# Weights that land in the place of their low parts, and VectorE's order in time mixing, in a one-layer RWKV and feed-forward kernel

## The chip, the cores and the metric

The kernel runs on one core of one Trainium2 chip. The metric is the device time of one execution in microseconds; lower is better. The five compute engines are named as the profile names them: PE (TensorE), DVE (VectorE), ACT (ScalarE), POOL (GpSimd), SP (SyncE, which here issues DMAs). An SBUF tile of 128 partitions by 512 fp32 elements is 256 KB.

## What is computed

```
x  = layernorm(x0) (no gain)            # then, on that x:
h  = LN(x)*g1 + b1;  hh = h shifted by one token (first row 0)
k  = (h*mk + hh*(1-mk)) @ Wk.T          # v with mv and Wv, r with mr and Wr
wkv = a / b of the first step of the recurrence (from k, v, tm_first)
x1 = x + (sigmoid(r) * wkv) @ Wo.T
h2 = LN(x1)*g2 + b2;  hh2 = h2 shifted
kv = silu((h2*ck + hh2*(1-ck)) @ Wkey.T) @ Wval.T
x2 = x0 + x1 + sigmoid((h2*cr + hh2*(1-cr)) @ Wcr.T) * kv
out = x2 + (silu(z @ Wg.T) * (z @ Wu.T)) @ Wdown.T,   z = layernorm(x2)
```

There are 2048 tokens, 512 features, and an inner width of 2048. Wr, Wk, Wv, Wo and Wcr are 512 x 512, all fp32.

## The kernel before, in words

**Precision.** Each fp32 operand of a matmul is split into two parts. The high part is what ScalarE's copy into a float32r tile leaves (`ACT.Copy`); the low part is the raw value minus the high part, a `tensor_tensor` subtract. Each product takes three passes: high x high, high x low, low x high (lines 488 to 490). A 512 x 512 weight matrix is four tiles ("items") of 128 x 512 and so costs four high copies on ScalarE and four low subtracts on GpSimd.

**Tokens** are worked in four blocks `b` of 512. Time mixing and the receptance of channel mixing come first (to about 285 us); then 48 "units" of the key, value and gated feed-forward products run to the end, and the change does not touch their code.

**TensorE's order in time mixing** is written out by hand: first_norm1 (transposes), receptance(0), key(0), norm1(1), value(0), and for b = 1 to 3: receptance(b), output(b-1), key(b), norm1(b+1) (or norm2(0)), value(b). Then norm2(1), channel_receptance(0), norm2(2), output(3), channel_receptance(1), norm2(3), channel_receptance(2) and (3). Each product is 48 matmuls of 128 x 512. `banks` A hold transposes, banks B hold products.

**The chain of one operand** (kind r, k, v, y or cr, block b): ScalarE's `rest_of` writes the shifted share from bank A into one of four ring tiles `made` (line 744); VectorE's `mix` adds the own share (lines 1097, 1099; the second is the first column alone, which takes its shifted share from `edge`); ScalarE's `operand_hi` makes the high part (line 733); GpSimd's `operand_lo` the low part (line 1409) and with it frees the ring tile. y has gated_value (line 1132) in the place of rest_of and mix.

**Every engine works strictly in the order of its own list**, and waits are semaphores. `receptance_gate` (sigmoid of bank B, line 761) frees bank B for the next product: key(0) waits for gate(0), and output(0) for gate(1). `wkv_weight(b)` is ScalarE's relu and two exps (lines 768 to 773) with VectorE's two products (lines 1121, 1124); it frees bank B for value(b).

**Weights.** Wr and Wk (items 0 to 7) are loaded to `held` at the start. Wv, Wo and Wcr go through a staging area of two tiles (`load`, line 378): SP loads item n once `item_done` says that GpSimd has made the low part of item n-2. ScalarE makes the high parts of Wv right after the mixing of k0, those of Wo after the mixing of r1, those of Wcr in block 3 before wkv_weight(3). `item_done` counts all low parts in one semaphore.

**The last token of a block** (`last_token`) goes to `edge`: four copies of one column from the bank (line 1078), a product with `rest_g` (line 1080) and an addition of the vector beta (line 1083), for all mixes at once.

**VectorE's order**: constants, first_norm1, mix r0, norm1_stats(1), mix k0, norm1(1), mix v0, last_token(0,0), norm1_stats(2), back_to_first, wkv_weight(0), norm1(2), mix r1, norm1_stats(3); then for each b: gated_value(b-1), mix k_b, mix v_b, last_token, (b = 1: norm1(3)), output(b-1), norm2_stats(b-1), wkv_weight(b), norm2(b-1), mix r_(b+1). GpSimd makes the inverse roots (`norm1`, `norm`: lines 1421, 1425) between its low parts.

## Time and profile before

| | us |
|---|---|
| median of 3 runs (1127.1 to 1129.96) | 1128.62 |
| the profiled execution's own time | 1127.89 |
| its span (first to last instruction) | 1126.1 |
| PE busy in it | 1063.3 (94%) |
| VectorE, ScalarE, GpSimd busy | 636.6, 485.6, 551.5 |

The profiled execution ran 1.8 us longer than its span and 0.7 us under the median. PE busy says how long a matmul was in flight, at whatever clock; its idle time is 63 us, most of it in the first 100 us.

### The profile page before, as it was taken

To read this page: it belongs to the slowest core of one execution; us is meant where nothing else is said; L and a number is where in the kernel's file an instruction comes from. 1 tells how busy PE (TensorE), PEld (TensorE's weight loads), DVE (VectorE), ACT (ScalarE), POOL (GpSimd) and SP (SyncE) were. 2 spreads that over 40 slices of the span, in tenths; PEclk is the share of its full clock that TensorE was granted. 3 is DMA by queue.
4 is the path that set the end of the run, shared out by engine and by line. 5 is a ranking of instruction groups with operands and counts; after the bars stand their busy time and mean duration, and the time that the engine had idled before them with its cause. 6 is when DMAs were issued, how large, how long until landed. Compare 5 with 4: busy or idle time off the path is not lost. (4 is left out here: it accounts for less than half of the span.)

```text
span 1126.1 us, 13091 instructions
## 1 busy us (share of the span) xinstructions
PE 1063.3 (94%) x4704; PEld 875.0 (78%) x4704; DVE 636.6 (57%) x1073; ACT 485.6 (43%) x807; POOL 551.5 (49%) x460
## 2 busy tenths in 40 slices
PE   4597999998999999999999999999998999999998
PEld 3476888877788887888877788887876788888887
DVE  6466574787344647556338556676659433333334
ACT  5456756766544345243334433333334222222221
POOL 5754537544575664355336465564644433333322
PEclk9798999999999999999999899999999999999999
DMA  6110203336853344635232266664446364444422
GB/s 245 38 38 0 39 1 64 68 125 223 326 181 128 123 168 149 188 126 191 85 102 100 98 224 225 224 208 142 162 181 208 94 222 150 143 147 150 146 80 75
DMA packets 45233, 157.18 MB, mean 140 GB/s; under 512 B 4080, under 2 KB 4208, under 8 KB 40560
## 3 DMA queue, kind: packets, MB, share of 16 engines
q1 hardware_dynamic: 30000, 108.10, 27.8%
q0 software_dynamic: 15168, 48.24, 14.3%
q8 instruction: 38, 0.62, 0.2%
q14 instruction: 27, 0.22, 0.1%
HBM read 97.60 MB, written 58.72 MB: 139 GB/s over the span
## 5 line engine op out<-in xcount | busy, mean ns | idle before, releaser
L1220 DVE TENSOR_TENSOR resid<-bank,resid 128x512 f32<-128x512 f32 x240 | 164.8, 689 | 244.3 <-PE bank L490 242.7
L499 PE MATMUL bank<-combo,left 128*128 128x512 f32 x672 | 264.1, 393 | 12.7 <-ACT bank L904 7.2
L1452 POOL TENSOR_TENSOR inner<-made,inner 128x512 fp32r<-128x512 f32 x128 | 167.5, 1330 | 219.8 <-ACT inner L859 219.5
L500 PE MATMUL bank<-combo,left 128*128 128x512 f32 x672 | 262.6, 391 | 0.0
L501 PE MATMUL bank<-combo,left 128*128 128x512 f32 x672 | 262.3, 390 | 0.0
L488 PE MATMUL bank<-right,inner 128*128 128x512 f32 x512 | 199.3, 389 | 0.0
L489 PE MATMUL bank<-right,inner 128*128 128x512 f32 x512 | 199.2, 389 | 0.0
L490 PE MATMUL bank<-right,inner 128*128 128x512 f32 x512 | 199.2, 389 | 0.0
L1430 POOL TENSOR_TENSOR left<-quart,left 128x512 fp32r<-128x512 f32 x96 | 116.7, 1237 | 104.8 <-ACT left L824 53.3
L499 PEld LDWEIGHTS bank<-combo,left 128*128 128x128 f32 x672 | 126.8, 189 | 42.9 <-ACT bank L904 8.5
L501 PEld LDWEIGHTS bank<-combo,left 128*128 128x128 f32 x672 | 126.8, 189 | 26.7
L500 PEld LDWEIGHTS bank<-combo,left 128*128 128x128 f32 x672 | 126.9, 189 | 25.9
L1447 POOL TENSOR_TENSOR right<-tall_staged,right 128x512 fp32r<-128x512 f32 x64 | 85.6, 1347 | 56.7 <-ACT right L837 56.7
L488 PEld LDWEIGHTS bank<-right,inner 128*128 128x128 f32 x512 | 96.1, 188 | 20.3 <-POOL inner L1452 0.4
L490 PEld LDWEIGHTS bank<-right,inner 128*128 128x128 f32 x512 | 96.1, 188 | 20.1
L489 PEld LDWEIGHTS bank<-right,inner 128*128 128x128 f32 x512 | 96.1, 188 | 19.9
L1409 POOL TENSOR_TENSOR operand<-made,operand 128x512 fp32r<-128x512 f32 x64 | 81.9, 1359 | 57.3 <-ACT operand L733 57.3
L880 ACT ACTIVATE made<-bank 128x512 f32<-128x512 f32 x64 | 38.0, 593 | 150.4 <-PE bank L501 150.4
L488 PE MATMUL bank<-operand,weights 128*128 128x512 f32 x176 | 70.1, 398 | 14.2 <-ACT held L761 13.5
L1097 DVE SCALAR_TENSOR_TENSOR made<-bank,whole_g,made 128x511 f32<-128x511 f32 x64 | 47.6, 744 | 55.8 <-ACT made L744 55.8
L868 ACT ACTIVATE made<-bank 128x512 f32<-128x512 f32 x64 | 37.5, 586 | 95.9 <-PE bank L501 95.9
L859 ACT ACTIVATE inner<-made 128x512 fp32r<-128x512 f32 x128 | 77.2, 628 | 2.7 <-ACT made L868 0.4
(130 smaller groups left out, 1464.2 us busy)
## 6 DMA issues: line engine op xcount, KB each, us to landing
kept_left<-left SPq DMA_DIRECT2D x24, 1792.0 KB, 8.1
left<-kept_left POOLq DMA_DIRECT2D x24, 1024.0 KB, 7.1
left<-kept_left POOLq DMA_DIRECT2D x24, 768.0 KB, 5.0
tall_staged<-tall SPq DMA_DIRECT2D x64, 256.0 KB, 3.3
quart<-wide SPq DMA_DIRECT2D x24, 512.0 KB, 4.2
raw<-kept SPq DMA_DIRECT2D x32, 256.0 KB, 6.4
resid<-x POOLq DMA_DIRECT2D x4, 1024.0 KB, 9.2
kept<-resid SPq DMA_DIRECT2D x4, 1024.0 KB, 5.8
```

What stands on the lines that cost most here:

```text
L488: pe.matmul(acc, left(0), right(0), start=first, stop=False)
L489: pe.matmul(acc, left(0), right(1), start=False, stop=False)
L490: return pe.matmul(acc, left(1), right(0), start=False, stop=last)
L499: pe.matmul(acc[:], hi, combo[:, c, k, 0, :], start=fresh and k == 0, stop=False, skip_group_check=True)
L500: pe.matmul(acc[:], hi, combo[:, c, k, 1, :], start=False, stop=False, skip_group_check=True)
L501: mm = pe.matmul(acc[:], lo, combo[:, c, k, 0, :], start=False, stop=k == 1, skip_group_check=True)
L859: act.activation(inner[:, h % 4, i, 0, :], made_at(n), ACT.Copy).then_inc(inner_hi, 1)
L1220: dve.tensor_tensor(tile, A[s][:], tile, ALU.add).then_inc(added, 1)
L1409: pool.tensor_tensor(place(kind, b, k, 1), made[:, (n + k) % RING, :], place(kind, b, k, 0).bitcast(F32), ALU.subtract).then_inc(op_lo, 1)
L1430: lo = pool.tensor_tensor(left[u % 2][:, 1, a[0]:a[0] + n, :], quart[:, a[0] + 1:a[0] + 1 + n, :], left[u % 2][:, 0, a[0]:a[0] + n, :].bit ...
L1447: pool.tensor_tensor(right[:, g % 2, i, 1, :], tall_staged[i][:], right[:, g % 2, i, 0, :].bitcast(F32), ALU.subtract).then_inc(right_lo, 1)
L1452: pool.tensor_tensor(inner[:, h % 4, i, 1, :], made_at(n), inner[:, h % 4, i, 0, :].bitcast(F32), ALU.subtract).then_inc(inner_lo, 1)
```

## The change

- The raw tile of every weight item is loaded straight into the place of its low part in `weights` (`landed`, the same memory as fp32). ScalarE reads it there, and the low part is written over it. The staging area and its waits are gone. SP issues the 16 items of Wr, Wk, Wv before block 1's tokens, Wo after them, then blocks 2 and 3. Wcr takes the rows of Wr and is loaded once receptance(3) is done.
- The low parts of Wk, of Wv and of the last tile of Wr move from GpSimd to VectorE. Those of Wo stay on GpSimd, at the same place; those of Wcr on GpSimd move from before `norm(BLOCKS + 2)` in block 3 to just before the low part of cr0, and its high parts on ScalarE from before wkv_weight(3) to behind it.
- `item_done` becomes one semaphore for each matrix.
- The small vectors are loaded second, behind the first token tile; `constants()` runs inside first_norm1.
- VectorE's order: the r-tile and Wk's first two tiles around mix r0 and mix k0, then Wk's other two, norm1_stats(1), Wv's four, norm1(1), mix v0, last_token, wkv_weight(0), norm1_stats(2), back_to_first, mix r1. norm1(2) and norm1(3) move to between mix k_b and mix v_b of blocks 1 and 2; norm1_stats(3) moves behind last_token of block 1.
- `last_token` makes each edge column in one instruction from the bank (12 or 8 tiny ones in the place of 6).
- ScalarE does channel_receptance(1) before, and no longer behind, the high parts of T2 and of unit 0's left factors.

```diff
-STAGES = 2
-EARLY = ITEM_V
+ROWS = 16
...
+        landed = at("landed", AT_WEIGHTS, [P, ROWS, 2, 512])
...
         def landing(item):
-            return early(item) if item < EARLY else staging[:, item % STAGES, :]
+            return landed[:, item % ROWS, 1, :]
...
-            def load(item, source):
-                if item >= EARLY + STAGES:
-                    sp.wait_ge(item_done, item - STAGES + 1)
-                sp.dma_start(staging[:, item % STAGES, :], source).then_inc(staged[item % STAGES], 16)
+            def load(items):
+                for item in items:
+                    sp.dma_start(landing(item), wts[item]).then_inc(w_loaded[item], 16)
...
-            for n in range(SUBS):
+            sp.dma_start(resid[:, 0, 0], x_blocks[0][:, 0, :]).then_inc(x_first[0], 16)
+            sp.dma_start(vec[:], vectors).then_inc(vec_loaded, 16)
+            for n in range(1, SUBS):
                 sp.dma_start(resid[:, 0, n], x_blocks[0][:, n, :]).then_inc(x_first[n], 16)
-            sp.dma_start(vec[:], vectors).then_inc(vec_loaded, 16)
             sp.dma_start(ident[:], identity).then_inc(ident_loaded, 16)
-            load_early(range(ITEM_R, ITEM_K))
+            load(range(ITEM_R, ITEM_O))
             sp.dma_start(resid[:, 1], x_blocks[1]).then_inc(x_loaded[0], 16)
-            load_early(range(ITEM_K, ITEM_V))
+            load(range(ITEM_O, ITEM_CR))
             for b in range(2, BLOCKS):
                 sp.dma_start(resid[:, b], x_blocks[b]).then_inc(x_loaded[b - 1], 16)
-            for item in range(ITEM_V, ITEMS):
-                load(item, wts[item])
+            sp.wait_ge(r_psum, KT * BLOCKS)
+            load(range(ITEM_CR, ITEMS))
```

On ScalarE:

```diff
-                if b + 1 == BLOCKS:
-                    act.wait_ge(r_psum, KT * BLOCKS)
-                    matrix_hi(ITEM_CR, ROW_CR)
                 wkv_weight(b)
                 if b + 1 < BLOCKS:
                     mixed("r", b + 1)
+            matrix_hi(ITEM_CR)
             mixed("cr", 0)
...
             combo_hi_of(0, T3)
+            channel_receptance(1)
             combo_hi_of(0, T2)
             unit_left_hi(0, 0)
             unit_left_hi(0, 1)
-            channel_receptance(1)
```

On VectorE:

```diff
                 for k in range(KT):
                     dve.wait_ge(transposed, KT * b + k + 1)
-                    dve.tensor_copy(last_z[:, n, k:k + 1], A[k][:, BT - 1:BT]).then_inc(last_taken, 1)
-                dve.wait_ge(last_taken, KT * (n + 1))
-                dve.tensor_tensor(edge[:, b, ms, :], rest_g[:, ms, :],
-                                  last_z[:, n:n + 1, :].broadcast_to(wide), ALU.mult).then_inc(edge_part, 1)
-                dve.wait_ge(edge_part, n + 1)
-                dve.tensor_tensor(edge[:, b, ms, :], edge[:, b, ms, :],
-                                  vec[:, beta:beta + 1, :].broadcast_to(wide), ALU.add).then_inc(edge_ready, 1)
+                    for m in ms:
+                        taken = dve.scalar_tensor_tensor(out=edge[:, b, m, k:k + 1], in0=A[k][:, BT - 1:BT],
+                                                         scalar=rest_g[:, m, k:k + 1], in1=vec[:, beta, k:k + 1],
+                                                         op0=ALU.mult, op1=ALU.add)
+                    taken.then_inc(last_taken, 1)
...
             def norm2_stats(b):
                 dve.wait_ge(x1_ready, SUBS * (b + 1))
+                dve.wait_ge(ln_rstd, BLOCKS - 1 + b)
...
             first_norm1()
             dve.wait_ge(const_done, 7)
+            last_of_r_lo()
             mix("r", 0)
+            matrix_lo(ITEM_K, range(2))
+            mix("k", 0)
+            matrix_lo(ITEM_K, range(2, KT))
             norm1_stats(1)
-            mix("k", 0)
+            matrix_lo(ITEM_V)
             norm1(1)
             mix("v", 0)
             last_token(0, 0)
+            wkv_weight(0)
             norm1_stats(2)
             for b in range(2):
                 back_to_first(b)
-            wkv_weight(0)
-            norm1(2)
-            back_to_first(2)
             mix("r", 1)
-            norm1_stats(3)
             for b in range(1, BLOCKS):
                 gated_value(b - 1)
                 mix("k", b)
+                if b + 1 < BLOCKS:
+                    norm1(b + 1)
+                    back_to_first(b + 1)
                 mix("v", b)
                 if b + 1 < BLOCKS:
                     last_token(0, b)
                 if b == 1:
-                    norm1(3)
-                    back_to_first(3)
+                    norm1_stats(3)
                 output(b - 1)
```

On GpSimd:

```diff
             first_norm1()
-            matrix_lo(ITEM_R, ROW_R, range(3))
-            operand_lo("r", 0, range(1))
-            matrix_lo(ITEM_R, ROW_R, range(3, KT))
-            operand_lo("r", 0, range(1, KT))
+            matrix_lo(ITEM_R, range(KT - 1))
+            operand_lo("r", 0)
+            operand_lo("k", 0)
             norm1(1)
-            matrix_lo(ITEM_K, ROW_K)
-            operand_lo("k", 0)
-            matrix_lo(ITEM_V, ROW_V)
             operand_lo("v", 0)
             norm1(2)
             operand_lo("r", 1)
-            norm1(3)
-            matrix_lo(ITEM_O, ROW_O)
+            matrix_lo(ITEM_O)
             for b in range(1, BLOCKS):
                 operand_lo("y", b - 1)
                 operand_lo("k", b)
                 operand_lo("v", b)
-                if b + 1 == BLOCKS:
-                    matrix_lo(ITEM_CR, ROW_CR)
+                if b == 1:
+                    norm1(3)
                 norm(BLOCKS + b - 1)
                 if b + 1 < BLOCKS:
                     operand_lo("r", b + 1)
                 x_added(b - 1)
+            matrix_lo(ITEM_CR)
             operand_lo("cr", 0)
```

## Rows read from the trace of the kernel before

**Rows 1.** Who waited longest for whom: TensorE, 0 to 330 us (line, releaser: total, times, longest)
```profile
PE bank L488 <- ACT held L761: 21.0, 2, 13.5
```

**Rows 2.** Windows 10 to 20, 40 to 50, 260 to 280 us: length, busy by engine, PEclk, DMA share, GB/s
```profile
10.00:20.00 10.00, 5.87 (x20) 4.04 (x21) 8.10 (x21) 5.78 (x11) 7.63 (x8) 1.00 1.05 387
40.00:50.00 10.00, 5.12 (x13) 4.06 (x14) 3.01 (x7) 8.31 (x14) 2.97 (x3) 0.53 0.34 95
260.00:280.00 20.00, 18.58 (x76) 15.29 (x77) 14.17 (x28) 17.50 (x31) 9.62 (x8) 0.91 0.74 223
```

**Rows 3.** Timeline of TensorE, 18 to 91 us (start, length, engine line, idle before and releaser)
```profile
18.57 0.76 PE L517 MATMUL bank<-operand,weights 128*128 128x512 f32 x1 [2.84 <-ACT operand L733]
...
44.88 0.80 PE L488 MATMUL bank<-operand,weights 128*128 128x512 f32 x1 [13.54 <-ACT held L761]
...
57.99 1.91 PE L552 MATMUL bank<-ident,resid 128*128 128x128 f32 x16
...
71.56 0.50 PE L488 MATMUL bank<-operand,weights 128*128 128x512 f32 x1 [0.71 <-DVE made L1132]
...
90.23 0.80 PE L488 MATMUL bank<-weights,operand 128*128 128x512 f32 x1 [7.50 <-ACT held L761]
```

**Rows 4.** Timeline of ScalarE, 40 to 57 us
```profile
40.91 0.63 ACT L719 ACTIVATE weights<-staging 128x512 fp32r<-128x512 f32 x1 [12.14 <-DMA staging<-wts]
...
42.94 1.28 ACT L761 ACT_TABLE_LOAD   x1
...
50.89 0.71 ACT L768 ACTIVATE bank<-bank,minus_bonus 128x512 f32<-128x512 f32 x1
...
56.35 0.60 ACT L771 ACTIVATE e<-bank 128x512 f32<-128x512 f32 x1 [1.66 <-DVE held L1121]
```

**Rows 5.** DMAs in flight at 1.8 to 2.5 us (count, KB each, median us from issue to landing)
```profile
resid<-x SPq DMA_DIRECT2D x2, 256.0 KB, 4.1
```

**Rows 6.** Timeline of VectorE, 6 to 64 us
```profile
6.66 0.17 DVE L1002 TENSOR_SCALAR minus_bonus<-vec 128x4 f32<-128x4 f32 x1 [6.66 <-DMA vec<-vectors]
...
8.86 0.68 DVE L1031 BATCH_NORM_STATS2 moments<-resid 128x6 f32<-128x512 f32 x1
...
12.40 2.15 DVE L1063 TENSOR_SCALAR resid<-resid,stats,rstd 128x512 f32<-128x512 f32 x2 [0.25 <-POOL rstd L1415]
...
62.02 1.90 DVE L1063 TENSOR_SCALAR resid<-resid,stats,rstd 128x512 f32<-128x512 f32 x4
```

**Rows 7.** Groups by line and form on VectorE, 0 to 280 us (busy, mean ns, idle before)
```profile
L1097 DVE SCALAR_TENSOR_TENSOR made<-bank,whole_g,made 128x511 f32<-128x511 f32 x64 | 47.6, 744 | 55.8 <-ACT made L744 55.8
L1048 DVE BATCH_NORM_STATS2 moments<-resid 128x6 f32<-128x512 f32 x28 | 17.3, 679 | 0.1
...
L1099 DVE SCALAR_TENSOR_TENSOR made<-bank,whole_g,edge 128x1 f32<-128x1 f32 x48 | 10.0, 208 | 0.0
...
L1083 DVE TENSOR_TENSOR edge<-edge,vec 128x12 f32<-128x12 f32 x3 | 3.6, 1212 | 0.1
```

**Rows 8.** Timeline of VectorE at 847 us, where GpSimd worked too
```profile
847.58 3.47 DVE L1188 TENSOR_TENSOR raw<-raw,raw 128x512 f32<-128x512 f32 x2
```

**Rows 9.** Timeline of GpSimd, 65 to 225 us
```profile
65.75 5.07 POOL L1409 TENSOR_TENSOR operand<-made,operand 128x512 fp32r<-128x512 f32 x4 [8.96 <-ACT operand L733]
...
80.35 4.99 POOL L1409 TENSOR_TENSOR operand<-made,operand 128x512 fp32r<-128x512 f32 x4
...
219.26 5.07 POOL L1409 TENSOR_TENSOR operand<-made,operand 128x512 fp32r<-128x512 f32 x4 [3.33 <-ACT operand L733]
```

**Rows 10.** Channel mixing: TensorE (two), ScalarE, and a DMA in flight at 275 us
```profile
245.41 0.50 PE L488 MATMUL bank<-weights 128*128 128x512 f32 x1 [2.29 <-DVE resid L1144]
...
261.42 0.79 PE L488 MATMUL bank<-weights 128*128 128x512 f32 x1 [3.09 <-ACT raw L812]
...
260.79 2.04 ACT L812 ACTIVATE raw<-bank 128x512 f32<-128x512 f32 x4
...
quart<-wide SPq DMA_DIRECT2D x1, 512.0 KB, 10.1
```

More of the change, by code:

```diff
@@ L319, in build @@
         x_loaded = [sem(f"x_loaded{b}") for b in range(1, BLOCKS)]
-        early_loaded = [sem(f"early_loaded{n}") for n in range(EARLY)]
+        w_loaded = [sem(f"w_loaded{n}") for n in range(ITEMS)]
         raw_kept = [sem(f"raw_kept{n}") for n in range(2)]
@@ L325, in build @@
         gate_kept = [sem(f"gate_kept{b}") for b in range(BLOCKS)]
-        staged = [sem(f"staged{n}") for n in range(STAGES)]
         w_hi = sem("w_hi")
-        item_done = sem("item_done")
+        item_lo = [sem(f"item_lo{n}") for n in range(ITEMS // KT)]
+        last_r_lo = sem("last_r_lo")
         const_done = sem("const_done")
@@ L1112, in mix_ck, with last_of_r_lo, matrix_lo @@
                                              in1=first_column(b, m, k), op0=ALU.mult, op1=ALU.add).then_inc(ck_made, 1)
+            def last_of_r_lo():
+                row = KT - 1
+                dve.wait_ge(w_hi, row + 1)
+                dve.tensor_tensor(weights[:, row, 1, :], landing(row), weights[:, row, 0, :].bitcast(F32),
+                                  ALU.subtract).then_inc(last_r_lo, 1)
+            def matrix_lo(item, tiles=range(KT)):
+                for k in tiles:
+                    row = (item + k) % ROWS
+                    dve.wait_ge(w_hi, item + k + 1)
+                    dve.tensor_tensor(weights[:, row, 1, :], landing(item + k), weights[:, row, 0, :].bitcast(F32),
+                                      ALU.subtract).then_inc(item_lo[item // KT], 1)
             def wkv_weight(b):
```

71 lines of the change are left out of this document (30 added, 41 removed).

## The prediction, made before the changed kernel ran

> **What bounds the kernel now.** I read TensorE's waits first: one line holds 21.0 us in two waits, the longest 13.5, both for the sigmoid that frees a product bank [rows 1]. TensorE's timeline places them: key(0) starts at 44.88 after 13.54 us idle, output(0) at 90.23 after 7.50 [rows 3]. From there to channel mixing the view of the waits lists no gap, so a microsecond gained before output(0) is gained at the end, as long as each block's operands keep coming. ScalarE's timeline tells why the sigmoid is late: at 40.91 it had waited 12.14 us for a staged tile of Wv, and the sigmoid's table load at 42.94 was behind that tile in its list [rows 4]. The tile had room only once GpSimd had made the low part of the tile two before it. The hole costs twice: the granted clock was 0.53 over 40 to 50 us [rows 2], and key(0) took 44.88 to 57.99, 13.1 us in place of the 11 or so that a product of 48 matmuls takes at full clock (receptance(1) ran from 71.56 to 82.73, where output(0)'s wait begins, the last matmul's tail of some 0.2 in it: 10.9 from start to start) [rows 3].
>
> **The change, part by part.** All times are of the profiled execution (1127.9; span 1126.1).
>
> *Start.* VectorE waits for the small vectors until 6.66 [rows 6]. From the third token tile's statistics (8.86) to the end of the last normed tile (12.40 + 2.15 = 14.55) it takes 5.7 us. The third tile is issued at about 1.6 and such tiles land 4.1 later [rows 5], at 5.7; with 0.7 us for constants() in the middle (an estimate: seven tiny instructions like the one at 6.66, whose 0.17 overlap by half) the last normed tile ends at 5.7 + 5.7 + 0.7 = 12.1. Gain 2.4; bounds 0 (another wait of the same length) and 3.1 (constants free). Wr's high parts don't depend on this and are done before. receptance(0) moves from 18.57 to 16.1 and ends at 28.7 (31.3 before).
>
> *The first hole.* Weights: SP's queue moved 387 GB/s over 10 to 20 us [rows 2]. Behind 1.1 MB of block 0 come Wr, Wk, Wv (3.1 MB) and block 1 (1 MB), so Wv is there at about 15 and block 1 at 18; ScalarE wants Wv at 25.5 and VectorE block 1 at 28. Both are covered, by 7 us at least. Nothing then stands between Wv's high parts (to 27.6) and the sigmoid: the first bank is ready at 28.05, table load 1.28, sigmoid 0.6, and key(0) starts at 30.0 in the place of 44.88. A hole of 1.3 us should keep the clock: after a wait of 2.29 the first matmul took 0.50 us, after those of 3.09 and 7.50 it took 0.79 and 0.80, as a cold one does [rows 10, 3]. So key(0) ends at 40.9 (57.99 before).
>
> *VectorE's new tiles.* It makes nine low parts, 0.68 us each alone. With GpSimd at work a subtract of two SBUF tiles took 3.47 / 2 = 1.73 us [rows 8], and GpSimd's own slows from 1.27 to as much. Five of the nine (Wr's last, Wk's four) meet GpSimd's low parts of r0 and k0, so I take 1.73 for these; for Wv's four, when GpSimd is idle but for one root, 0.78. Bounds 0.64 and 1.73 for all nine. On the path: Wr's last ends at 13.8 beside ScalarE's r0 work, no loss. Wk 0 and 1 end at 21.5, mix k0 at 24.5 (four times 0.744 and a column, 3.15 [rows 7]), Wk 2 and 3 at 28.1, norm1_stats(1) at 31.3 (3.2: four of 0.679 and the rest [rows 7]), Wv at 34.4, norm1(1) at 36.3 (1.9, as at 62.02 [rows 6]), mix v0 at 39.4, last_token at 40.8.
>
> The Trainium skill's page "SBUF — State Buffer", section "SBUF: two separate sides", speaks against this part: a VectorE instruction with two SBUF inputs and a GpSimd instruction that reads SBUF take an exclusive lock for the whole instruction, and the later one fully blocks. By that rule each met tile would cost a whole GpSimd tile and its own, about 1.96 us, and the forecast would be half a microsecond later; the measured pair is shorter than the sum of the two. The same rule explains why the edge's addition (two SBUF inputs, 12 elements) took 1.212 us in each of its cases [rows 7]; the new edge columns have one SBUF tensor input each.
>
> *From there to output(0)* the chain is no longer TensorE's. ScalarE's exps of k0 begin at 40.0 (high parts of v0 behind mix v0), and from their start (50.89) to VectorE's last product (62.02) it was 11.1 us [rows 4, 6], of which 1.66 were ScalarE waiting for a late VectorE (at 56.35 [rows 4]); so 49.5. Then norm1_stats(2) with back_to_first, 3.8, which now stand directly before mix r1: mix r1 begins at 53.3, GpSimd's low parts of r1 at 54.9 (1.6 behind, as now: norm1(2) ends at 63.9 with mix r1 right behind it, the low parts begin at 65.75 [rows 6, 9]). They take 5.1, Wo's four 5.1 without a wait (in before they were stretched to 80.35 by staging), and from the start of y0's low parts (80.35) to output(0) (90.23) it is 9.9 us by GpSimd, ring, mixing of k1 and sigmoid [rows 9, 3]. Sum: 54.9 + 5.1 + 5.1 + 9.9 = 75.0 against 90.23: **15.2 us gained**. TensorE meanwhile: value(0) 44.0 to 54.9, then waits 2.2 for y0's first tile (0.71 before [rows 3]) and 0.7 for r1's low parts, receptance(1) ends at 68.9, and a hole of 6.1 us stays before output(0), with its cold clock. What is late next is thus mix r1 and the three sets of low parts in GpSimd's row.
>
> *Blocks 1 to 3.* norm1(b+1) before mix v_b meets the low parts of k_b: up to 5.9 us (four tiles of 1.47) for 1.9. In block 1 VectorE reaches output(0) at 85.5 (norm1(2) to 77, mix v1 80.5, last_token 1.4, norm1_stats(3) 3.2); TensorE needs the bank at 75.0 + 12.5 = 87.5. Covered by 2. The new wait on ln_rstd in norm2_stats(0) is for GpSimd's root behind v1's low parts, about 87: hidden by output(0) itself (88). I take 0; if the cover is gone, each microsecond over 2 is paid once. last_token: twelve columns like those of line 1099, 0.208 each alone [rows 7]; they overlap, and between 0.7 and 2.5 I take 1.4, for about 1.9 now (four copies, the product, and the 1.212 of line 1083 [rows 7]): nothing here, since VectorE then awaits ScalarE.
>
> *Wcr.* Its load waits for receptance(3) and lands 20 us before use; keep_x1(0) behind it in SP's queue leaves earlier than now. But high parts (2.2) now stand before cr0's on ScalarE and low parts (5.1) before cr0's on GpSimd, behind x_added(2). In old times: cr0's low parts end at 221.0 (they end at 219.26 - 3.33 = 215.9 now), y3's start at 221.0 in the place of 219.26 [rows 9], and ring, cr1, sigmoids of cr0 and output(3) follow 1.7 later; the shorter last_token returns 0.3. **Loss 1.4**; bounds 0 and 5.1.
>
> *channel_receptance(1) earlier.* Before, its sigmoids at 260.79 were behind high parts that wait for VectorE, and channel_receptance(2) started at 261.42 after 3.09 idle [rows 10], with the clock at 0.91 over 260 to 280 us [rows 2], 1.8 us lost. Done early, both go: 4.9. Then the next limit: ScalarE reaches the sigmoids of cr2 only 0.7 after TensorE wants the bank, and at unit 0 the DMA queue, whose 512 KB of the next factors already took 10.1 us [rows 10], and x_added(3) before it move with the 1.4 above. There 3.0 of the 4.9 are left over and the DMAs set the rest. **Gain 3.0**; bounds 0 and 4.9.
>
> Sum: 15.2 - 1.4 + 3.0 = 16.8. 1127.9 - 16.8 = 1111.1 for a profiled execution, and as that of before was 0.7 under the median, **1111.8**.
>
> **Rivals.**
> 1. *The lock costs nothing* and cr's shift hides: low parts at 0.68 move the chain 3 us earlier (mix v0 at 36.4): 1108.5. For it: GpSimd pauses between tiles; against it, rows 8. Chance 0.12.
> 2. *Wcr is paid in full*: GpSimd is the limit of channel mixing, all 5.1 us appear and the earlier sigmoids gain nothing: 1128.6 - 15.2 + 5.1 = 1118.5. For it: operand_lo is one serial row through r, y and cr with the ring of four behind it. Against: 3.33 us idle before y3's [rows 9]. Chance 0.16.
> 3. *The hole only changes its name*: block 1's tokens, now behind three matrices, hold VectorE in norm1_stats(1), and with it Wv, norm1(1) and v0. It decides if they land after 28 us; to take all it needs 43, a quarter of the measured rate: 1127. Chance 0.03.
> 4. *Slower*: VectorE is the limit in every block. Its list before output(b-1) got norm1(b+1) in contention (+4.0), in block 1 the statistics (+3.2). From the point where it reaches output(0) behind TensorE's 87.5, TensorE waits, cools and the lag feeds v_b and r_(b+1) of the next block. With 8 us in each of three blocks (6 of wait, 2 of clock) it is 1128.6 - 16.8 + 24 = 1136. Against: the sixteen mixings of VectorE waited 55.8 us in all for ScalarE [rows 7]. Chance 0.03.
>
> **How the numbers follow.** Forecast 0.66, rivals 0.12, 0.16, 0.03, 0.03. The range goes from 1106 (rival 1 with the start's upper bound) to 1119 (rival 2). A difference under 0.3%, 3.4 us, is about what a measurement of this kernel can't tell from none; rivals 3 and 4 alone are near or beyond it: faster 0.94, same 0.03, slower 0.03.
>
> **What would show it.** In the changed profile: key(0) at 30 with 1 to 2 us idle and clock 1.0; the last normed tile of block 0 near 12.1; VectorE's Wk tiles at 1.7, Wv's near 0.7; a hole of 6 us before output(0) at 75, released by the sigmoid; no stall at key(1); no idle time on GpSimd between Wcr's, cr0's and y3's low parts; no wait on the sigmoid of line 812 over 1 us. I am wrong if output(0) starts after 78 or before 72, or if TensorE has a gap over 1 us in blocks 1 to 3.

## The result, and the profile after

The changed kernel takes **1109.92 us** (median of four runs, 1109.02 to 1111.04) against 1128.45 for the kernel before in the same comparison: a ratio of 0.9836 [0.9819, 0.9853], 18.5 us less. The forecast was 1111.8 with a range of 1106 to 1119. The profiled execution is the slowest of the four (1111.04; span 1109.2), and against the profiled execution before (1127.89) it gains 16.9 us, where the sum said 16.8. So the terms are compared between the two profiles, and the totals between medians. How far one execution can stray is told behind the experiments.

All line numbers below are of the changed kernel (an experiment's can be a few lines off): products 479 to 481, norm1 1050, mix 1080 and 1082, VectorE's low parts 1100 and 1107, gated_value 1128, output 1140, last_token 1064, rest_of 730, high parts 714 and 719, gate 747, GpSimd's low parts 1392 (weights) and 1404 (operands).

Who waited for whom, TensorE of the changed kernel, 0 to 330 us (total, times, longest), answers to [rows 1]:

```profile
PE bank L555 <- DVE resid L1050: 10.1, 3, 9.4
PE bank L479 <- ACT held L747: 5.7, 1, 5.7
PE bank L511 <- ACT operand L719: 2.9, 1, 2.9
PE bank L490 <- ACT made L854: 2.5, 1, 2.5
```

Of the line that held 21.0 us one wait of 5.7 is left, and the wait for the sigmoid of channel mixing is gone from the list (waits of 2.1 and less follow behind these four). TensorE's timeline of the changed kernel, 30 to 279 us, has the places that were forecast (start, length, and in brackets the idle time before), beside [rows 3, 10]:

```profile
30.02 1.07 PE L515 MATMUL bank<-operand,weights 128*128 128x512 f32 x4
31.10 0.50 PE L479 MATMUL bank<-operand,weights 128*128 128x512 f32 x1
...
56.03 0.50 PE L479 MATMUL bank<-operand,weights 128*128 128x512 f32 x1 [1.08 <-DVE made L1128]
...
73.66 0.79 PE L479 MATMUL bank<-weights,operand 128*128 128x512 f32 x1 [5.67 <-ACT held L747]
...
200.55 1.91 PE L547 MATMUL bank<-ident,held 128*128 128x128 f32 x16
...
230.22 0.50 PE L479 MATMUL bank<-weights 128*128 128x512 f32 x1 [2.09 <-DVE resid L1140]
...
278.82 0.76 PE L490 MATMUL bank<-combo,left 128*128 128x512 f32 x1 [2.53 <-ACT made L854]
```

What the reader is to see: key(0) starts at 31.10 on the heels of receptance(0), where it started at 44.88 after 13.54 idle; output(0) at 73.66 in the place of 90.23; channel_receptance(1) at 230.22 in the place of 245.41; the matmul of unit 0 that waits for ScalarE's `made` at 278.82 (296.54 in the trace before). The gain against before at these four places is thus 13.8, 16.6, 15.2 and 17.7 us, and 16.9 at the end.

The windows of the changed kernel (length, busy by engine, clock, DMA share, GB/s), for [rows 2]:

```profile
40.00:50.00 10.00, 10.00 (x54) 8.50 (x53) 7.04 (x13) 9.77 (x16) 2.08 (x2) 1.00 0.00 1
60.00:90.00 30.00, 24.33 (x100) 19.64 (x99) 22.10 (x55) 14.35 (x23) 20.95 (x17) 0.89 0.00 1
90.00:200.00 110.00, 110.00 (x511) 91.77 (x511) 72.92 (x163) 76.86 (x120) 53.64 (x43) 1.00 0.23 46
230.00:234.00 4.00, 3.78 (x10) 2.98 (x11) 3.96 (x8) 0.35 (x1) 0.00 (x0) 0.62 1.00 376
278.00:282.00 4.00, 3.17 (x8) 2.48 (x9) 0.00 (x0) 3.83 (x8) 4.00 (x4) 0.59 1.00 302
```

Between 90 and 200 us TensorE is busy for all 110 us: neither VectorE nor GpSimd became the limit in blocks 1 to 3. The clock is 1.00 over 40 to 50 us, where it was 0.53, and low after three waits: 5.67, 2.09 and 2.53.

VectorE of the changed kernel, 5 to 85 us, for [rows 6, 7, 8]:

```profile
5.71 0.69 DVE L1016 BATCH_NORM_STATS2 moments<-resid 128x6 f32<-128x512 f32 x1 [1.51 <-DMA resid<-x]
...
7.13 0.69 DVE L1016 BATCH_NORM_STATS2 moments<-resid 128x6 f32<-128x512 f32 x1 [0.40 <-DMA resid<-x]
...
11.26 2.15 DVE L1050 TENSOR_SCALAR resid<-resid,stats,rstd 128x512 f32<-128x512 f32 x2 [0.25 <-POOL rstd L1410]
13.33 1.75 DVE L1100 TENSOR_TENSOR weights<-landed,weights 128x512 fp32r<-128x512 f32 x1
...
19.44 2.73 DVE L1107 TENSOR_TENSOR weights<-landed,weights 128x512 fp32r<-128x512 f32 x2 [1.22 <-ACT weights L714]
...
25.23 3.10 DVE L1107 TENSOR_TENSOR weights<-landed,weights 128x512 fp32r<-128x512 f32 x2
...
31.18 2.50 DVE L1107 TENSOR_TENSOR weights<-landed,weights 128x512 fp32r<-128x512 f32 x4
...
83.78 2.06 DVE L1140 SCALAR_TENSOR_TENSOR resid<-resid,back,bank 128x512 f32<-128x512 f32 x3
```

The nine new tiles took 1.75, a pair in 2.73, a pair in 3.10 beside GpSimd's, and four in 2.50 alone. Taken singly, the second tile of the first pair and the GpSimd tile that it met are

```profile
20.40 1.77 DVE L1107 TENSOR_TENSOR weights<-landed,weights 128x512 fp32r<-128x512 f32 x1
```

```profile
19.89 1.73 POOL L1404 TENSOR_TENSOR operand<-made,operand 128x512 fp32r<-128x512 f32 x1
```

GpSimd's tile ends at 21.62 and VectorE's 0.55 later, at 22.17. The other three of Wk took 1.04, 1.40 and 1.78 and ended 0.55 behind a GpSimd tile too (at 19.93, 26.08 and 27.78). GpSimd of the changed kernel, 53 to 209 us, for [rows 9]:

```profile
53.77 5.03 POOL L1404 TENSOR_TENSOR operand<-made,operand 128x512 fp32r<-128x512 f32 x4 [0.40 <-ACT operand L719]
58.74 5.04 POOL L1392 TENSOR_TENSOR weights<-landed,weights 128x512 fp32r<-128x512 f32 x4
63.73 5.04 POOL L1404 TENSOR_TENSOR operand<-made,operand 128x512 fp32r<-128x512 f32 x4
...
193.89 5.56 POOL L1392 TENSOR_TENSOR weights<-landed,weights 128x512 fp32r<-128x512 f32 x4
...
203.91 5.47 POOL L1404 TENSOR_TENSOR operand<-made,operand 128x512 fp32r<-128x512 f32 x4
```

Both rows of three are there as forecast, without a pause: r1, Wo, y0 ahead of output(0), and Wcr, cr0, y3 in block 3. Last, ScalarE of the changed kernel, at the first gate and ahead of unit 0, for [rows 4, 10]:

```profile
28.37 1.28 ACT L747 ACT_TABLE_LOAD   x1
30.45 2.07 ACT L747 ACTIVATE held<-bank 128x512 f32<-128x512 f32 x4 [0.80 <-PE bank L515]
...
271.45 0.85 ACT L810 ACTIVATE left<-quart 128x768 fp32r<-128x768 f32 x1 [1.50 <-DMA quart<-wide]
274.56 1.27 ACT L823 ACTIVATE right<-tall_staged 128x512 fp32r<-128x512 f32 x2 [2.26 <-DMA tall_staged<-tall]
```

At 28.37 the table load ran before the wait for TensorE's bank, not behind it. Before unit 0 ScalarE waits twice for transfers.

### The profile page after: what moved, and what is told of

Same layout as the page of the kernel before. It is cut to its first block and busy times, and to the rows that moved or that the text cites. A ratio compares the mean times of both kernels' runs of the same rounds, so it can differ in the third digit from the quotient of the medians.

```text
span 1109.2 us, 13090 instructions
## 1 busy us (share of the span) xinstructions
PE 1065.0 (96%) x4704; PEld 875.0 (79%) x4704; DVE 641.9 (58%) x1106; ACT 485.7 (44%) x807; POOL 542.1 (49%) x451
## 5 line engine op out<-in xcount | busy, mean ns | idle before, releaser
L1404 POOL TENSOR_TENSOR operand<-made,operand 128x512 fp32r<-128x512 f32 x64 | 84.9, 1425 | 44.2 <-ACT operand L719 44.2
L1280 DVE TENSOR_TENSOR made<-bank,made 128x512 f32<-128x512 f32 x64 | 44.0, 690 | 58.5 <-ACT made L866 37.1
```

The costliest lines, as they stand in the source:

```text
L1404: pool.tensor_tensor(place(kind, b, k, 1), made[:, (n + k) % RING, :], place(kind, b, k, 0).bitcast(F32), ALU.subtract).then_inc(op_lo, 1)
```

## The experiments

Each kernel is told by the median of its four runs, with its ratio to the kernel before, which ran beside it and had medians of 1127.6 to 1128.5. Unless it says otherwise an edit is made to the changed kernel.

**The landing alone, on the kernel before.** All else is as before: low parts, VectorE's order, last_token, vectors, Wcr's place, the late sigmoids. In diff against the changed kernel, cut to two of its places:

```diff
-            sp.dma_start(vec[:], vectors).then_inc(vec_loaded, 16)
             for n in range(1, SUBS):
                 sp.dma_start(resid[:, 0, n], x_blocks[0][:, n, :]).then_inc(x_first[n], 16)
+            sp.dma_start(vec[:], vectors).then_inc(vec_loaded, 16)
...
+                if b + 1 == BLOCKS:
+                    act.wait_ge(r_psum, KT * BLOCKS)
+                    matrix_hi(ITEM_CR)
                 wkv_weight(b)
...
```

> The kernel before with nothing changed but the landing of the weights: all low parts on GpSimd, VectorE's order, the edge, the sigmoids, Wcr's places and the order of the first loads as before. If the landing carries the change: key(0) starts near 33 us, the low parts of Wv and Wo have no gaps for a load, output(0) starts near 76.5 in the place of 90.2, and the time is 1113 to 1115, three quarters of the gain. If the new orders are needed for most of it: 1119 or more.

Measured: 1114.46 (1114.41 to 1118.86), ratio 0.9885 [0.9864, 0.9905]; three of its runs lie within 0.1 us of each other, the fourth is the 1118.86. TensorE of this kernel, 33 to 79 us:

```profile
33.30 0.47 PE L480 MATMUL bank<-operand,weights 128*128 128x512 f32 x1 [1.96 <-POOL operand L1406]
...
63.02 0.66 PE L480 MATMUL bank<-operand,weights 128*128 128x512 f32 x1 [3.27 <-DVE made L1133]
...
78.99 0.50 PE L480 MATMUL bank<-weights,operand 128*128 128x512 f32 x1 [3.17 <-ACT held L748]
```

The landing alone brings output(0) from 90.23 to 78.99 and gives 1.15% of the 1.64% of the whole change: 70%, by its interval between 58 and 83%. The 13.5 us hole was the staging area's, not GpSimd's load. What its own low parts leave behind shows as small waits at key(0) (2.9 in four), a wait of 3.27 for y0, and a later row (its r1 low parts start at 57.27; 53.77 in the changed kernel).

**The nine low parts back on GpSimd,** with the landing and the rest kept. norm1_stats(1) had to go ahead of mix k0, since GpSimd's root now stands there:

```diff
             dve.wait_ge(const_done, 7)
-            last_of_r_lo()
             mix("r", 0)
-            matrix_lo(ITEM_K, range(2))
-            mix("k", 0)
-            matrix_lo(ITEM_K, range(2, KT))
             norm1_stats(1)
-            matrix_lo(ITEM_V)
+            mix("k", 0)
             norm1(1)
...
-            matrix_lo(ITEM_R, range(KT - 1))
-            operand_lo("r", 0)
+            matrix_lo(ITEM_R, range(3))
+            operand_lo("r", 0, range(1))
...
+            operand_lo("r", 0, range(1, KT))
+            norm1(1)
+            matrix_lo(ITEM_K)
             operand_lo("k", 0)
-            norm1(1)
+            matrix_lo(ITEM_V)
             operand_lo("v", 0)
```

> The changed kernel, but with the nine low parts of Wr's last tile, Wk and Wv back on GpSimd and VectorE's norm1_stats(1) before mix k0 again; the weights still land in the place of their low parts. If landing without staging is what removed the first hole, and the low parts' engine is second: GpSimd's row (root, Wk's four, k0's four) lets key(0) start near 33 us in the place of 31.1, with some 3 us idle or slow steps before it, and Wv's follow under key(0); output(0) starts near 75, the time is 1110 to 1113. If moving the nine tiles to VectorE was needed for the gain (they are 12 us of GpSimd's row ahead of v0), key(0) or value(0) waits for them and the time is 1117 to 1121.

Measured: 1111.08 (1110.34 to 1111.83), ratio 0.9853 [0.9838, 0.9867], 1.2 us over the changed kernel with intervals that overlap. GpSimd of this kernel, Wk's and k0's low parts, with Wv's (35.09) and v0's (40.10 to 46.5) behind them:

```profile
24.43 5.40 POOL L1388 TENSOR_TENSOR weights<-landed,weights 128x512 fp32r<-128x512 f32 x4
29.79 5.35 POOL L1400 TENSOR_TENSOR operand<-made,operand 128x512 fp32r<-128x512 f32 x4
```

GpSimd makes all four sets in a row in 22 us while TensorE works on receptance(0) and key(0). It costs key(0) 2.38 and 0.49 us of waits, and VectorE is free earlier in return: output(0) starts at 72.82, inside the 72.6 to 74.2 of the traces whose code is that of the changed kernel up to there. Moving the tiles is worth about 1 us, if anything. Between this kernel and the landing alone lie the rest of VectorE's order, last_token, the start, Wcr and the sigmoids: together 3.4 us (1114.46 - 1111.08), 6.2 at output(0). VectorE's order by itself was not taken back in any run, so its own share is not shown.

**Wo's parts early:** its high parts behind the shifted share of v0, its low parts behind v0's low parts, when GpSimd is idle for 9.65 us.

```diff
             receptance_gate(0)
-            mixed("v", 0)
+            rest_of("v", 0)
+            matrix_hi(ITEM_O)
+            mix_hi("v", 0)
             wkv_weight(0)
             mixed("r", 1)
-            matrix_hi(ITEM_O)
...
             operand_lo("v", 0)
+            matrix_lo(ITEM_O)
             norm1(2)
             operand_lo("r", 1)
-            matrix_lo(ITEM_O)
```

> The changed kernel with Wo earlier: high parts on ScalarE between rest_of v0 and the high parts of v0, low parts on GpSimd directly behind those of v0, where GpSimd idles 9.7 us. If the hole of 5.7 us before output(0) is the four low parts of Wo standing between those of r1 and those of y0 (the forecast's chain), y0's low parts start right behind r1's, 4 us earlier after 1 us lost on v0's high parts; the hole is 1 to 2 us, the clock stays up (1.6 more), and the time is 1104 to 1106. If the hole is set by ScalarE's ring, mixing and sigmoid alone, it stays at 5 us or more and the time is 1109 to 1111.

Measured: 1103.97 (1102.67 to 1104.29), ratio 0.9787 [0.9773, 0.9802]: 6 us under the changed kernel. Its timelines of GpSimd and of TensorE, and its window of 60 to 90 us:

```profile
42.01 6.86 POOL L1393 TENSOR_TENSOR weights<-landed,weights 128x512 fp32r<-128x512 f32 x4
...
53.49 10.01 POOL L1405 TENSOR_TENSOR operand<-made,operand 128x512 fp32r<-128x512 f32 x8 [0.40 <-ACT operand L719]
```

```profile
68.41 0.50 PE L479 MATMUL bank<-weights,operand 128*128 128x512 f32 x1 [0.71 <-ACT held L747]
```

```profile
60.00:90.00 30.00, 29.29 (x129) 23.73 (x129) 25.87 (x62) 20.10 (x31) 16.80 (x13) 1.00 0.00 1
```

r1's and y0's low parts now follow each other directly; the hole shrinks from 5.67 to 0.71 and the clock no longer falls (1.00 against 0.89). So the second half of the forecast's chain is shown: output(0) hung on GpSimd's row, and Wo's 5.04 us stood in it.

**Wcr's parts where they were before:** high parts ahead of wkv_weight(3), low parts behind v3's.

```diff
                 mixed("v", b)
+                if b + 1 == BLOCKS:
+                    matrix_hi(ITEM_CR)
                 wkv_weight(b)
...
-            matrix_hi(ITEM_CR)
             mixed("cr", 0)
...
+                if b + 1 == BLOCKS:
+                    matrix_lo(ITEM_CR)
                 norm(BLOCKS + b - 1)
...
-            matrix_lo(ITEM_CR)
             operand_lo("cr", 0)
```

> The changed kernel with Wcr's high and low parts in their old places in block 3 (before wkv_weight(3), and before the root of norm2(2)); its load stays. If Wcr's low parts ahead of cr0's cost 1.4 us by the chain y3, cr1, sigmoids, output(3): y3's low parts start 1.7 us earlier, the transposes of norm2(2) take 2.5 in the place of 3.4 us, and the time is 1108.5. If VectorE's right_sums(0) ahead of output(3) is the limit, the wait before channel_receptance(1) grows by what is saved in front of it and the time stays at 1110.

Measured: 1107.07 (1106.11 to 1108.23), ratio 0.9817 [0.9803, 0.9832], 2.9 us under the changed kernel, 1.9 under its repetition below; the intervals touch, but each of its four runs is under each of the eight of those two. The traces tell Wcr's share apart from what came earlier, by the stretch from the transposes of norm2(1) to channel_receptance(1). It starts at 200.55 in the changed kernel; in this kernel and in the kernel before at

```profile
199.70 1.91 PE L547 MATMUL bank<-ident,held 128*128 128x128 f32 x16
```

```profile
217.03 1.91 PE L552 MATMUL bank<-ident,held 128*128 128x128 f32 x16
```

and ends at 230.22, 226.90 and 245.41 [rows 10]: 29.7 us in the changed kernel, 27.2 here, 28.4 before. So Wcr's place costs 2.5, not 1.4, and something else in the change gives 1.2 back (the old last_token with Wcr early, below, tells what). Part of the gain goes into a new wait of 1.6 for the sigmoids of channel mixing.

**The sigmoids of channel_receptance(1) late, as before:**

```diff
             combo_hi_of(0, T3)
-            channel_receptance(1)
             combo_hi_of(0, T2)
...
             unit_left_hi(0, 1)
+            channel_receptance(1)
             mixed("cr", 3)
```

> The changed kernel with channel_receptance(1)'s sigmoids back behind the high parts of T2 and of unit 0's left factors. If the early sigmoids took away the wait before channel_receptance(2): that wait comes back with 3 us and, unless the clock is lucky, 1.7 us of slow matmuls; 3.0 of it reach the end, 1113. If unit 0's DMAs set the end of this stage anyway: the wait comes back, but the wait in unit 0 (2.5 us) goes down by as much and the time is 1110.

Measured: 1111.61 (1109.2 to 1112.78), ratio 0.9861 [0.9844, 0.9877], 1.7 us over the changed kernel; the intervals overlap, and the number lies between the two theories. Its waits of TensorE (a third at unit 0, for VectorE's bank, has 1.0):

```profile
PE bank L490 <- ACT made L854: 1.6, 2, 0.8
...
PE bank L479 <- ACT raw L798: 0.7, 1, 0.7
```

With late sigmoids the wait is 0.7, not the 3.1 of before, and the landing alone, whose sigmoids are late too, has the same 0.7. In both the product ahead of it ran slow at its start (clock 0.66 over 230.5 to 235.5 us here, 1.00 at that place in the kernel before), and these 1.6 us went into the wait. Unit 0's waits (1.6 + 1.0) are as long as the 2.5 of the changed kernel. So the 3.0 that the sum gave to this edit weren't its own; its size stays open between 0 and 3, and the part on the forecast below narrows it by the traces.

**The vectors in fifth place, as before:**

```diff
-            sp.dma_start(vec[:], vectors).then_inc(vec_loaded, 16)
             for n in range(1, SUBS):
                 sp.dma_start(resid[:, 0, n], x_blocks[0][:, n, :]).then_inc(x_first[n], 16)
+            sp.dma_start(vec[:], vectors).then_inc(vec_loaded, 16)
```

> The changed kernel with the small vectors loaded fifth again, behind the four token tiles. The changed profile shows the second tile's statistics at 5.7 us and the third's at 7.1, later than the 4.0 and 5.7 at which they could have begun before. If the many small packets of the vectors hold the token tiles up, these come back to about 4.0 and 5.7, the constants wait for 6.6, the last normed tile ends near 12.3 (13.4 now) and the time falls by about 1 us, to 1109. If the token tiles' landing only varies from run to run, they stay late or the same, and the time stays at 1110 or rises by up to 1.

Measured: 1109.79 (1108.74 to 1110.42), ratio 0.9833 [0.9818, 0.9847]: no difference in the time. VectorE of this kernel, from 3 us:

```profile
3.44 1.32 DVE L1016 BATCH_NORM_STATS2 moments<-resid 128x6 f32<-128x512 f32 x2 [3.44 <-DMA resid<-x]
...
5.00 0.69 DVE L1016 BATCH_NORM_STATS2 moments<-resid 128x6 f32<-128x512 f32 x1
```

The second token tile is there by the end of the first one's statistics (4.1, against 5.71), the vectors at 5.95, and the last normed tile ends at 11.6 in the place of 13.4. In the ten traces with the vectors second, the second tile's statistics begin at 5.2 to 6.1, so the delay is theirs and not chance. receptance(0) starts at 15.71 in the place of 17.47 (16.4 to 17.5 in those ten) and output(0) at 71.91 in the place of 73.66, which the median of four runs doesn't repeat. In place of a gain, the second place of these 20 KB delayed the tokens; the start was gained by constants() no longer standing ahead of all statistics.

**The old last_token** (four copies, product, addition) in the changed kernel:

```diff
                 for k in range(KT):
                     dve.wait_ge(transposed, KT * b + k + 1)
-                    for m in ms:
-                        taken = dve.scalar_tensor_tensor(out=edge[:, b, m, k:k + 1], in0=A[k][:, BT - 1:BT],
-                                                         scalar=rest_g[:, m, k:k + 1], in1=vec[:, beta, k:k + 1],
-                                                         op0=ALU.mult, op1=ALU.add)
-                    taken.then_inc(last_taken, 1)
+                    dve.tensor_copy(last_z[:, n, k:k + 1], A[k][:, BT - 1:BT]).then_inc(last_taken, 1)
+                dve.wait_ge(last_taken, KT * (n + 1))
+                dve.tensor_tensor(edge[:, b, ms, :], rest_g[:, ms, :],
+                                  last_z[:, n:n + 1, :].broadcast_to(wide), ALU.mult).then_inc(edge_part, 1)
...
```

> The changed kernel with last_token in its old form (four copies, a product and an addition). If its length lies beside waits for ScalarE everywhere but in channel mixing, where 0.3 us of it count: 1110 to 1110.5. If the addition's wait for GpSimd (1.2 us in each) is on the path in blocks 0 and 1: 1111 to 1112.

Measured: 1115.95 (1113.82 to 1117.08), ratio 0.9886 [0.9871, 0.9901]. 6 us slower than the changed kernel, far from what was expected. VectorE, GpSimd and TensorE of this kernel, 194 to 209 us:

```profile
196.64 8.02 DVE L1068 TENSOR_TENSOR edge<-rest_g,last_z 128x8 f32<-128x8 f32 x1
204.70 0.17 DVE L1071 TENSOR_TENSOR edge<-edge,vec 128x8 f32<-128x8 f32 x1
```

```profile
194.20 5.54 POOL L1397 TENSOR_TENSOR weights<-landed,weights 128x512 fp32r<-128x512 f32 x4
199.22 5.41 POOL L1409 TENSOR_TENSOR weights<-made,weights 128x512 fp32r<-128x512 f32 x4
```

```profile
205.75 3.32 PE L548 MATMUL bank<-ident,held 128*128 128x128 f32 x16 [4.74 <-issue]
```

A product of 128 x 8 elements with two SBUF inputs lasted 8.02 us: from 196.64 to 204.66, and GpSimd's row of eight subtracts, Wcr's four and cr0's four, ended at 204.63. TensorE's transposes came 5.2 us later than in the changed kernel (200.55). The new edge columns at this place, eight in 1.09 us, have one SBUF tensor each (the other input is the bank, the factor one SBUF column) and passed through the same row.

**The old last_token with Wcr early,** the two edits above together, to tell whether it is the old form or its meeting with that row:

> The changed kernel with both the old last_token and the old places of Wcr's high and low parts in block 3. In the run with the old last_token alone, one product of eight elements took 8.02 us on VectorE in block 0 of channel mixing, from 196.64 to the end of GpSimd's row of eight low parts (Wcr's four and cr0's four). If that row starves the small product, then with Wcr's low parts out of the row the product waits for at most what is left of cr0's four, as in the kernel before (0.3 to 0.8 us), and the time is 1107 to 1108, that of Wcr early alone. If the old edge costs in itself, the time is 1112 to 1113.

Measured: 1108.99 (1107.03 to 1109.96), ratio 0.9834 [0.9804, 0.9864]. VectorE and GpSimd of this kernel:

```profile
196.34 0.81 DVE L1069 TENSOR_TENSOR edge<-rest_g,last_z 128x8 f32<-128x8 f32 x1
197.18 1.21 DVE L1072 TENSOR_TENSOR edge<-edge,vec 128x8 f32<-128x8 f32 x1
```

```profile
194.51 5.09 POOL L1410 TENSOR_TENSOR weights<-made,weights 128x512 fp32r<-128x512 f32 x4
```

The same instruction, also in the middle of a row of subtracts, took 0.81. The old form costs 6.0 us where Wcr's low parts adjoin cr0's (1115.95 - 1109.92); with Wcr early it costs 1108.99 - 1107.07 = 1.9. Read the other way, moving Wcr costs 7.0 with the old form (1115.95 - 1108.99) and 2.9 with the new one (1109.92 - 1107.07). So the two edits belong together: **without the new edge columns, moving Wcr would have cost 4 us more.** The stretch from norm2(1) to channel_receptance(1) is 28.4 us here and 27.2 with the new columns: they are the 1.2 that was given back.

**right_sums(0) behind output(3):** the 2.09 wait at 230.22 is for VectorE's output(3), and its list has right_sums(0) ahead of that.

```diff
             mix_ck(2)
-            right_sums(0)
             output(BLOCKS - 1)
             norm2_stats(BLOCKS - 1)
+            right_sums(0)
             combo_lo_of(0, B11)
```

> The changed kernel with right_sums(0) behind output(3) and norm2_stats(3) on VectorE, not ahead of them. If the wait of 2.1 us before channel_receptance(1) is these four subtracts ahead of output(3), it goes, the clock is no longer at risk there (1.65 us in the profiled run), the DMAs behind norm2(3) start earlier too, and the time is 1107 to 1108. If unit 0's DMAs set the end of channel mixing, the wait goes but comes back in unit 0: 1110.

Measured: 1107.62 (1106.84 to 1108.25), ratio 0.9814 [0.9797, 0.983]: 2.3 us less than the changed kernel, 1.4 less than its repetition. The wait is gone from the view of the waits, and two others stand in its place (2.0 for the sigmoid of line 798, 1.3 for norm2(3)); what remains is the late channel mixing that went with it.

**The three moves together** (Wo early, Wcr early, right_sums late), **and with the vectors in fifth place:**

Of the three moves:

> The changed kernel with three moves together: Wo early, Wcr early, right_sums(0) late. If their gains stand at different waits they add: 5.9 for Wo, 2.8 for Wcr, and for right_sums what its own run shows of 2 us, less what overlaps with Wcr: 1098 to 1101. If channel mixing is set by unit 0's DMAs, Wcr and right_sums give nothing on top of each other: 1102.

Of the four:

> The same three moves with the small vectors loaded fifth again. If the start is on the chain to output(0) and the vectors' place costs 1 us: 1 us under the kernel with three moves. If not: the same.

Measured: 1100.58 (1099.37 to 1101.9), ratio 0.9761 [0.9736, 0.9786], and 1100.97 (1099.98 to 1101.6), ratio 0.9766 [0.9737, 0.9794]. Both beat the kernel before by 27 us and the changed kernel by 8 to 9. TensorE's waits of the three moves:

```profile
PE bank L479 <- ACT raw L798: 2.0, 1, 2.0
...
PE bank L547 <- DVE held L1156: 1.5, 1, 1.5
```

Alone they gave 6.0, 2.9 and 2.3, together 9.3 of 11.2: the last two both end in the same wait for the sigmoids of channel mixing (1.6 and 2.0 alone, 2.0 together), which may be where the rest went. The fourth brings output(0) from 69.55 to 68.01 and again nothing in the time.

**The changed kernel once more,** in the comparison with these two:

> The changed kernel itself once more, beside the kernels with three and four moves, for the spread of one kernel's traces: the same time as in its first runs, 1109 to 1111. If the slow clock behind the wait before channel_receptance(1) is chance, it may be there or not; the statistics of the second token tile at 5.7 us should come back if the small vectors cause them.

Measured: 1108.99 (1108.77 to 1110.91), ratio 0.9839 [0.9814, 0.9864], with output(0) at 74.23 after 5.66. Two medians of one kernel stand 0.9 us apart; differences of about 1 us between medians above are no more than that. The second token tile's statistics begin at 5.79 again, and the clock is 1.00 where it had been 0.62 and 0.59.

**One place in all traces.** Behind the changed stages TensorE meets the same wait of 2.03 us (for VectorE's `raw`) in every kernel. Its end, in one execution of each, and the clock in the window 540 to 575 us around it:

| | end of the wait, us | clock |
|---|---|---|
| before | 567.70 | 0.95 |
| landing alone | 554.10 | 0.95 |
| changed; once more | 550.59; 550.63 | 0.95; 0.95 |
| low parts on GpSimd | 550.51 | 0.95 |
| sigmoids late | 550.65 | 1.00 |
| vectors fifth | 549.07 | 0.95 |
| right_sums late | 549.48 | 1.00 |
| Wcr early | 547.14 | 0.95 |
| Wo early | 543.39 | 0.95 |
| three moves; four | 543.13; 541.30 | 1.00; 1.00 |
| old last_token; with Wcr early | 555.64; 548.46 | 0.95; 0.95 |

By this place the landing alone has 13.6 of the change's 17.1 us, and the old last_token costs 5.1 and 1.3. From here to the end no kernel differs in its code, yet the four executions whose clock stayed at 1.00 took 556.4 to 557.0 us and the others 558.4 to 558.8. So about 1.1 of the 2.3 us of right_sums late had come about before this place. The three moves are here only 0.3 ahead of Wo early alone (their output(0) came 1.1 later, 69.55 against 68.41); the medians put them 3.4 us ahead of it, and how much of that is Wcr's and right_sums' and how much the clock's is not shown.

## Why the prediction was right, step by step

**The bound** was read rightly. The staging area held Wv back, Wv held the sigmoid, and nothing in between hid it: the landing alone removes it.

**Start: mis-sized.** Forecast: last normed tile at 12.1, gain 2.4. Measured: 11.26 + 2.15 = 13.4, and receptance(0) 1.1 earlier. The step that failed is "the third tile lands at 5.7": its statistics began at 7.13, behind the vectors in the queue (5.00 with the vectors in fifth place).

**First hole: mis-sized by 1.3, the other way.** The sum put the table load behind the bank. It ran at 28.37, while the bank was still being filled, so the sigmoid followed the bank directly and key(0) had no hole at all. The two errors cancel almost. key(0) at 31.10 is still 1.1 behind the forecast 30.0, because receptance(0) itself took 13.6 us and not 12.6: one group of four of its matmuls took 1.88, where such a group took 1.07 in the trace before. 13.8 were gained.

**VectorE's tiles: a little under the forecast.** Forecast 1.73 met and 0.78 alone, 11.8 for the nine; measured 10.1, with 1.04 to 1.78 for a met tile and 0.62 alone. By the Trainium skill, page "SBUF — State Buffer", section "SBUF: two separate sides", a met tile waits for the whole instruction of the other engine. This trace agrees: each of the four Wk tiles ended 0.55 behind a GpSimd tile, about its own length alone. The prediction took the rule for half a microsecond more than its price by [rows 8]; it came out cheaper because the first tile of each pair met a GpSimd tile already under way (1.04 and 1.40). Mix v0 came at 35.42 (36.3), last_token took 1.59 (1.4), the exps began at 39.21 (40.0).

**Chain to output(0): right.** Mix r1 at 52.15 (forecast 53.3), r1's low parts 53.77 (54.9), Wo's 58.74 and y0's 63.73, each 5.04 without a pause, output(0) 9.9 behind y0's at 73.66 (75.0), hole 5.67 (6.1), released by the sigmoid. Every distance was met within 0.3. Of the 1.3 us, 0.9 came ahead of mix v0 (Wv's four tiles alone 0.6), 0.3 in the statistics, the rest in the row. Gain 16.6 for 15.2. Wo early shows what this row cost: 6 us.

**Blocks 1 to 3: right.** The cover of 2 us held: VectorE reached output(0) at 83.78 (forecast 85.5) and after three tiles waited 0.77 for TensorE's last bank. norm1(2) in contention took 5.55 (forecast 5.9).

**Wcr: right to the digit, by luck.** 16.6 at output(0) and 15.2 at channel_receptance(1) make a loss of 1.4. The row of three is there without a pause, as the step said. But the sum had 1.7 for the row and 0.3 back from the shorter last_token; by the stretch from norm2(1) on they are 2.5 and 1.2, and two errors of 0.8 and 0.9 cancelled.

**last_token: the step was wrong where the sum wasn't.** It said "nothing here", for the time of the instructions themselves. The row it meets in block 3 makes the old form cost 6.0 in the new order, where it costs 1.9 with that row short. The prediction had both pieces, the contention of two-input instructions and GpSimd's new row, and didn't put them together, since it costed the edge in the order of before.

**The early sigmoids: right sum, wrong share.** From 230.22 to unit 0 the kernel gained 2.5 (forecast 3.0), and DMA waits of 1.50 and 2.26 on ScalarE set the rest, as the step said. But kernels with late sigmoids gained it too. From channel_receptance(1) to the third of unit 0's waits, or its place (281.52 in the changed kernel), it was 53.5 us before, 51.2 with the landing alone, 51.3 with late sigmoids, 51.3 in the changed kernel and 49.6 in its repetition. The clock fell at the start of this stretch in the middle three and not in the last. So where it fell the early sigmoids gave nothing, and where it held they gave up to 1.7; the medians say 1.7 to 2.6. What the landing changed there is not shown, beyond the slow product that filled the wait.

**Clock: a term left out.** The wait at channel_receptance(1) had kept the clock before (2.29 us [rows 10]), and the sum had no term for losing it there. In the changed profile the matmuls fell to 0.63 us each from 231.09 to 234.1, about 1.7 us (eight matmuls 0.2 dearer each), and behind unit 0's wait the first took 0.76. In the repetition waits of 2.06 and 2.6 kept 1.00 in both windows. Yet that execution was as long (span 1109.1 against 1109.2): its slow stretch behind output(0) was longer (24.8 us from there to norm1(2)'s transposes, against 23.6), and it reached unit 0 within 0.1 us of the first. So this clock loss does not explain why the median gained 18.5 and the profile 16.9. Each of the two profiles is the slowest of its four runs; why stays open, and that the sum's 16.8 meets the 16.9 of one execution is luck as far as tenths go.

**Rivals.** The first (free contention): the tiles were cheaper than forecast, but mix v0 came 0.9 us earlier for it, not 3. The second (Wcr in full, 5.1) is refuted by the 2.5 measured. The third is refuted by the statistics of block 1 at 28.26 without a wait. (Ahead of block 1's tokens stand the twelve tiles of Wr, Wk and Wv, 3.1 MB, as the prediction has it; "The change" says 16. And 43 us would have needed a third of the measured rate, not a quarter: 5.2 MB in 39 us is 134 GB/s, against 387.) The fourth is refuted by the 110.00 busy of 110.

## What to carry to other kernels

Where a staged load holds up an engine's list, landing the data in the place of its own result takes the buffer and the wait away together, and most of the gain is there (70% by the medians); shifting nine tiles between engines afterwards brought 1 us at most. Then read the row of the engine whose work stands between the last producer and the next product, and move out of it what isn't urgent (Wo's four tiles: 6 us) into that engine's idle time. Before work is placed back to back on GpSimd, look for the small two-input VectorE instructions that will fall into that stretch: cost each edit in the order that the others make.

## What the runs showed of the hardware

- **A starved VectorE instruction.** A two-SBUF-input product of 128 x 8 lasted 8.02 us, to the end of eight GpSimd subtracts; in a row of four it took 0.81. The page "SBUF — State Buffer" of the Trainium skill (same section) has the later instruction blocked for one instruction of the other engine; the additions at 1.21 and Wk's 128 x 512 tiles agree with that, the 8.02 don't. GpSimd's subtracts start about 1.25 us apart in both rows, without a pause. In the row of eight each is on record for 1.7 to 1.8 us, so that the next has begun before it ends; in the row of four they last 1.32 to 1.37. Whether this or the length of the row decides wasn't tried.
- **Idle times of 2.0 to 2.6 us sometimes cost the clock and sometimes not:** 2.09 and 2.53 did in one execution of the changed kernel, 2.06 and 2.6 didn't in another, nor 2.29 in the kernel before. One wait of 2.03 that all kernels share left the clock at 1.00 in four of fourteen traces and at 0.95 over 35 us in the others.
- **The table load** ran ahead of a pending wait, and its 1.28 us vanished behind TensorE's work; behind it the next exp started at once (39.87 + 1.28, then 41.16). The Trainium skill's page "ScalarE: Activation LUTs", section "What ACT_TABLE_LOAD costs", gives 1.28 and a drain of 1.38 on top; no such pause is in this trace.
- **A 20 KB load** placed second in the queue let the next token tile's statistics begin at 5.2 to 6.1 us in ten traces, in the place of about 4.1, though by an estimate its bytes are worth 0.05 at the queue's later rate (393 GB/s over 10 to 20 us).
